# Row attention on one core: maxima rows ahead in the transfer queue, loads in two halves, and TensorE's shifted products ahead of its scores

## The reference

```python
def _L0_xattn_ref(q, k, v):
    b, d, m = q.shape            # 64, 64, 256
    h = N_HEAD                   # 8 heads of 8 rows
    qh = q.reshape(b * h, d // h, m)
    kh = k.reshape(b * h, d // h, -1)
    vh = v.reshape(b * h, c // h, -1)
    qk = jnp.einsum('bdm,bdn->bmn', qh, kh) * scale
    sm = jax.nn.softmax(qk, axis=-1)
    ret = jnp.einsum('bmn,bcn->bcm', sm, vh)
    return ret.reshape(b, c, m)

x = x + _L0_xattn_ref(_layernorm(x, axis=-1), ctx_2048, ctx_2048)
```

## Time and profile before

| what | value |
|---|---|
| median of 3 runs | 2517.65 us (2515.28 to 2520.46) |
| profiled execution | 2522.49 us, span of its trace 2520.6 us |
| mean granted TensorE clock | 0.792 of full |
| busy over the span | PE 60%, DVE 64%, ACT 42%, POOL 24% |
| row attention, first score to last result added | 146.6 us to 608.4 us |

### The profile page before, as it was taken

The page is one execution under the profiler, slowest core; times in us unless marked ns, Lnnn a source line. Parts: engine busy times, 40 slices in busy tenths (PEclk is TensorE's granted clock), DMA queues, the critical chain, the costliest instruction groups (busy, mean ns, idle before and its releaser), DMA issues. The chain is left out here.

```text
span 2520.6 us, 34997 instructions
## 1 busy us (share of the span) xinstructions
PE 1518.6 (60%) x11260; PEld 924.7 (37%) x11260; DVE 1622.3 (64%) x3141; ACT 1062.1 (42%) x1453; POOL 613.7 (24%) x862
## 2 busy tenths in 40 slices
PE   1069999994995787874334343279999367620022
PEld 1035555552774544542112112135555233310011
DVE  6457777773453477675777887445555487856787
ACT  4427667673221334344355455323333377710022
POOL 4312233332002223223333433201010011105500
PEclk9999999996998788897555556689999688855555
DMA  6635555542001221211000000001100100003001
GB/s 179 173 77 117 119 120 119 119 114 76 1 0 30 51 60 40 47 43 56 10 1 1 0 0 0 21 29 31 29 25 23 51 1 0 1 21 61 6 26 41
DMA packets 94652, 120.97 MB, mean 48 GB/s; under 512 B 25868, under 2 KB 78284, under 8 KB 89932
## 3 DMA queue, kind: packets, MB, share of 16 engines
q1 hardware_dynamic: 94540, 119.56, 19.0%
HBM read 79.75 MB, written 22.09 MB: 40 GB/s over the span
## 5 line engine op out<-in xcount | busy, mean ns | idle before, releaser
L571 DVE TENSOR_REDUCE ratt_nmax<-ratt_psS 128x2 f32<-128x512 f32 x512 | 319.9, 684 | 112.6 <-PE ratt_psS L463 112.0
L537 ACT ACTIVATE ratt_E<-ratt_psT 128x1024 f32<-128x1024 f32 x256 | 255.6, 1022 | 123.9 <-PE ratt_psT L485 123.8
L463 PE MATMUL ratt_psS<-ratt_K,ratt_Q 72*128 72x256 bf16 x1024 | 210.7, 291 | 54.4 <-DMA ratt_K<-ratt_ones 48.5
L485 PE MATMUL ratt_psT<-ratt_Q,ratt_K 75*128 75x256 bf16 x1024 | 202.6, 283 | 15.2 <-DMA ratt_Q<-ratt_rows 14.8
L498 PE MATMUL ratt_psO<-ratt_E,ratt_V 128*32 128x256 f32 x2048 | 144.8, 403 | 0.7 <-ACT ratt_E L537 0.7
L463 PEld LDWEIGHTS ratt_psS<-ratt_K,ratt_Q 72*128 72x128 bf16 x1024 | 82.3, 101 | 154.2 <-issue 94.0
L1833 PE MATMUL nffn_psH<-nffn_W,nffn_QT 128*128 128x512 bf16 x128 | 57.7, 601 | 114.6 <-DVE nffn_H L1797 95.8
L485 PEld LDWEIGHTS ratt_psT<-ratt_Q,ratt_K 75*128 75x128 bf16 x1024 | 102.4, 101 | 36.2 <-issue 16.8
L1316 PE MATMUL gatt_psA<-gatt_DA,gatt_same 128*128 128x512 f32 x128 | 89.1, 786 | 25.3 <-DVE gatt_DB L1201 25.3
L1135 POOL TENSOR_TENSOR gatt_DA<-gatt_own,gatt_a 128x1024 f32<-128x1024 f32 x32 | 61.5, 1935 | 143.4 <-PE gatt_psA L1319 90.4
L1756 POOL TENSOR_TENSOR nffn_H<-nffn_H,nffn_gam 128x1024 f32<-128x1024 f32 x32 | 93.1, 2937 | 7.4 <-DVE nffn_H L1788 7.4
(11 more groups left out here) (451 smaller groups left out, 4124.3 us busy)
## 6 DMA issues: line engine op xcount, KB each, us to landing
ratt_Q<-z_parts SPq DMA_DIRECT2D x32, 576.0 KB
ratt_K<-context_parts SPq DMA_DIRECT2D x96, 192.0 KB
gatt_V<-in_ctx_dram SPq DMA_DIRECT2D x16, 512.0 KB, 6.9
z_parts<-prep_ZS SPq DMA_DIRECT2D x48, 128.0 KB, 2.7
context_parts<-prep_CS SPq DMA_DIRECT2D x48, 128.0 KB
head_sums<-ratt_O SPq DMA_DIRECT2D x64, 72.0 KB
all_X<-in_x_dram SPq DMA_DIRECT2D x8, 512.0 KB, 4.8
prep_C<-in_ctx_dram SPq DMA_DIRECT2D x8, 512.0 KB, 5.6
```

Source lines behind the costliest of these rows:

```text
L463: mm = nc.tensor.matmul(psS[:, RING[h], c * D:(c + 1) * D], Q9[0:R, buf, h, k % 2, c * P:(c + 1) * P], K9[0:R, buf, h, k % 2, :], start=Tr ...
L485: mm = nc.tensor.matmul(psT[:, p % 2, e, c, :], K9[0:RM, buf, h, u, c * P:(c + 1) * P], Q9[0:RM, buf, h, u, :], start=True, stop=True)
L537: nc.scalar.activation(E[:, 2 * b + p // 2, 2 * (p % 2):2 * (p % 2) + 2], psT[:, p % 2], ACT.Exp, scale=SCALE).then_inc(exped, 1)
L571: nc.vector.tensor_reduce(nmax[:, k % 2, h, :], psS[:, RING[h]].rearrange("p (c t) -> p c t", c=2), AX.X, ALU.max, negate=True).then_inc(m ...
```

## The change

On SP the row comes first in each slot; the load is halved, with Q in the odd slot n and K in the even slot n+1 (group of units n+3 and n+4 as before, so K is issued one slot later than before); `inverses_out` moves from the pair's fourth slot to its next one (slot 4a+12), `back` from slot 4a+12 to 4a+14, behind that slot's K load. DVE's reciprocal goes from slot 4a+10 to 4a+11, POOL's `scale_and_add` from 4a+13 to 4a+15. The ones are all issued before the first load. On PE, each head's shifted product stands ahead of the score of the other unit's head.

```diff
                 def slot(i, k):
                     n = i * 8 + k
-                    row_there = held(sp, n) if is_unit(n - 1) else None
-                    if k % 2 == 1 and past(n, 5) and is_unit(n + 3):
-                        free = held(sp, n * 4 - 4 * LAG)
-                        pair = held(sp, i * 2 + (k + 3) // 4)
-                        sp.wait_ge(shifted, free)
-                        load(pair, (k + 3) // 2 % 2, (k + 3) // 2 % BUFS)
...
+                    if is_unit(n - 1):
+                        bring_row(held(sp, n), (k - 1) // 2 % BUFS, (k - 1) % 2)
+                    if past(n, 5):
+                        g = (k + 3) // 2 if k % 2 else (k + 2) // 2
+                        if is_pair(i * 2 + g // 2):
+                            if k % 2:
+                                free, pair = held(sp, n * 4 - 4 * LAG), held(sp, i * 2 + g // 2)
+                                sp.wait_ge(shifted, free)
+                                load_q(pair, g % 2, g % BUFS)
+                            else:
+                                load_k(held(sp, i * 2 + g // 2), g % 2, g % BUFS)
                     c = (k - 8) // 4
...
+                    if k % 4 == 0 and is_pair(i * 2 + c - 1):
+                        inverses_out(held(sp, (i * 2 + c - 1) * P), held(sp, i * 2 + c), (c - 1) % 2)
+                    if k % 4 == 0 and is_pair(i * 2 + c):
+                        out(held(sp, i * 2 + c), held(sp, (i * 2 + c) * 4 + 4), c % 2)
+                    if k % 4 == 1 and is_pair(i * 2 + c):
+                        sums_back(held(sp, (i * 2 + c) * 16), c % 2, held(sp, (i + c // 2) * 64 + 64))
+                    if k % 4 == 2 and is_pair(i * 2 + c - 1):
+                        back(held(sp, (i * 2 + c - 1) * 16), (c - 1) % 2, held(sp, (i + (c - 1) // 2) * 16 + 16))
...
                 for buf in range(BUFS):
                     sp.dma_start(K9[R:RM, buf].rearrange("p h u m -> p (h u) m"), spread(ones[:], 1, 2 * NH0)).then_inc(
                         ones_in, 16)
-                    load(buf // 2, buf % 2, buf)
-                slots(sp, slot, UNITS + 9)
+                for g in range(BUFS):
+                    load_q(g // 2, g % 2, g)
+                    load_k(g // 2, g % 2, g)
+                slots(sp, slot, UNITS + 11)
...
-                    c = (k - 13) // 4
-                    if k % 4 == 1 and is_pair(i * 2 + c):
+                    c = (k - 15) // 4
+                    if k % 4 == 3 and is_pair(i * 2 + c):
                         scale_and_add(i * 2 + c, c % 2, i + c // 2)
...
                         for e in range(2):
+                            if is_unit(m):
+                                shift(i, k, p, e)
                             if is_unit(n):
                                 score(i, k, 2 * p + e)
-                            if is_unit(m):
-                                shift(i, k, p, e)
...
-                    c = (k - 10) // 4
-                    if k % 4 == 2 and is_pair(i * 2 + c):
+                    c = (k - 11) // 4
+                    if k % 4 == 3 and is_pair(i * 2 + c):
                         dve.wait_ge(d_in[c % 2], (i + c // 2) * 16 + 16)
```

More of the change, by code:

```diff
@@ L319, in _, with load_q, load_k @@
             def _(sp):
-                def load(pair, b, buf):
+                def load_q(pair, b, buf):
                     q = zq.rearrange("s r a (b h) u m -> (s r) a b (h u m)", b=2)[:, bass.ds(pair, 1), b, :]
-                    k = ck.rearrange("r s a (b h) u m -> (r s) a b (h u m)", b=2)[:, bass.ds(pair, 1), b, :]
                     sp.dma_start(Q9[0:R, buf].rearrange("p h u m -> p (h u m)"), spread(
                         q.rearrange("p a m -> p (a m)"), 1, 3)).then_inc(group_in[buf], 16)
+                def load_k(pair, b, buf):
+                    k = ck.rearrange("r s a (b h) u m -> (r s) a b (h u m)", b=2)[:, bass.ds(pair, 1), b, :]
                     for part in range(3):
@@ L361, in slot @@
                     n = i * 8 + k
-                    row_there = held(sp, n) if is_unit(n - 1) else None
-                    if k % 2 == 1 and past(n, 5) and is_unit(n + 3):
-                        free = held(sp, n * 4 - 4 * LAG)
-                        pair = held(sp, i * 2 + (k + 3) // 4)
-                        sp.wait_ge(shifted, free)
-                        load(pair, (k + 3) // 2 % 2, (k + 3) // 2 % BUFS)
-                    ago = k % 4
-                    c = (k - 8) // 4
[L370 to L386, removed]
@@ L387, in slot @@
-                    if row_there is not None:
-                        bring_row(row_there, (k - 1) // 2 % BUFS, (k - 1) % 2)
+                    if is_unit(n - 1):
[9 more added lines that the diff above has]
+                                load_k(held(sp, i * 2 + g // 2), g % 2, g % BUFS)
@@ L441, in slot @@
                         split_max(n - 1, (k - 1) % 2)
-                    c = (k - 13) // 4
-                    if k % 4 == 1 and is_pair(i * 2 + c):
+                    c = (k - 15) // 4
+                    if k % 4 == 3 and is_pair(i * 2 + c):
                         scale_and_add(i * 2 + c, c % 2, i + c // 2)
-                slots(pool, slot, UNITS + 10)
+                slots(pool, slot, UNITS + 12)
             @block.tensor
@@ L582, in _ @@
                 nc.vector.tensor_copy(identb[:], ident[:]).then_inc(ident_set, 1)
-                slots(dve, slot, UNITS + 7)
+                slots(dve, slot, UNITS + 8)
 def pipeline(engine, front, back):
```

## The result

The changed kernel takes 2526.67 us (median of 7 runs, 2522.97 to 2537.0), the kernel before 2517.65 us beside it; the ratio is 1.0048 with a 95% interval of 1.0029 to 1.0067. So it is slower, as forecast and within the range of 2512 to 2600, but by 7 to 17 us (the medians lie 9 us apart, the ratio says 12) and not by 41. The wait that was forecast is there, twelve times and at the slots named. With what surrounds it, it cost 46.1 us, six tenths of the 75.6 in the sum.

The account below looks back on a forecast made before the run. PE's own stream was taken as the limit, with 31.7 us lost around late rows. The terms -31.7 + 75.6 + 4 - 7.3 + 1 = +41.6 us gave 2559 us from 2517.65, with 8 in 10 between 2512 and 2600.

Parts of the forecast that it names:

- Rows first, loads halved: On SP: rows no longer stand behind `back`'s wait or whole loads; PE's six waits and their clock go, -31.7 us.
- `back` behind K: POOL gets `num` late, so PE waits 3.5 us in twelve turns, with 2.8 us of lower clock each: +75.6 us.
- K one slot later: In even slots K's data end close to the first score's due time: 0.3 us in 12 slots, +4 us.
- Shifted product first: On PE: the new order moves everything by 0.22 us once and the slot stays 6.19 us: 0.
- Ones first: At the start PE begins at about 130 and slot 3 at 154 instead of 161.3: -7.3 us, -1 to -12.
- Tail: At the block's end the next to last pair's `back` stands between the last pair's `sums_back` and `inverses_out`: +1 us.
- Rival A: At POOL's wait: `num` is in time and no turn is late; -38 us, 2480 us, chance 0.12.
- Rival B: On the queue: `den` and `num` don't wait behind K; 1.8 us wait, 1.7 clock, +4, 2522 us, chance 0.12.
- Rival C: On PE: frequent waits leave the clock at 1.2 GHz for most of two slots; +74, 2592 us, chance 0.18.

Follow-up runs that it names:

- e1: The changed kernel with POOL's `scale_and_add` one POOL slot later, behind the split that a turn of PE waits for: 2481.11 us, ratio 0.9872.
- e8: The changed kernel with only the sum into X moved behind the next split, the product left in its POOL slot: 2491.34 us, ratio 0.9901.
- e9: The changed kernel with one more product of the same size, unused, on POOL ahead of the split: 2554.61 us, ratio 1.0162.
- e5: The kernel of e1 with PE's order of before, scores ahead of shifted products: 2481.56 us, ratio 0.9856.
- e2: The changed kernel with PE's order of before, scores ahead of shifted products: 2525.81 us, ratio 1.0048.
- e3: The kernel before with only PE's order changed, shifted products ahead of scores: 2517.04 us, ratio 1.0012.
- e4: The changed kernel with the ones issued in turn with the four first loads, as before: 2535.07 us, ratio 1.0081.
- e7: The kernel before with only the ones issued ahead of the four first loads: 2505.69 us, ratio 0.9948.
- r1: The changed kernel as it is, timed and profiled once more: 2527.41 us, ratio 1.0054.
- e6: The changed kernel with `back` (`den` and `num`) issued ahead of its slot's K load instead of behind it: 2551.14 us, ratio 1.0143.

## Why the prediction was wrong

By its own steps:

- *Rows first, loads halved, -31.7.* Right. In e1, where nothing else disturbs, all 31.7 us are back. Rows first and the halved loads were never run apart, so which of the two did it is open.
- *`back` behind K, 12 waits, +75.6.* The mechanism, the slots and the count were right; **this term was mis-sized**, at 46.1 us. Of the 29.5 us between, the wait itself is 42.0 - 27.5 = 14.5: `num` came at t = 10.55 instead of 11.3, mostly because `den` was issued at t = 4.34 and not at 4.9, while the distance from there to POOL's start was 6.21 us where 6.4 was taken (on the mean of the twelve `num` came at 10.3, 6.0 us behind `den`); and the 3.5 us ran from the due time of the turn, whereas PE waits less than it is late (2.63 us of 2.80 at slot 24) and makes up 0.34 us in the next slot. The other 15.0 us are the clock: 2.8 us were put behind each wait, 33.6 in all, and 18.6 were found. This is the step that failed: 12 x (3.5 + 2.8) took a wait of 3.5 us where 2.3 came, and a fall of the clock behind every one where only five had one. The six waits that this came from were 1.5 to 3.1 us long and all had a fall behind them. At the new place the clock fell behind 5 of 12 waits of 2.3 us, behind none of 0.9 (e8), and behind all twelve of 3.6 (e9). The length alone doesn't explain it, as the last section shows: waits for rows of the same 2.3 us always had a fall.
- With waits as long as forecast the loss is about as forecast: e9 has 3.6 us, twelve falls and 70.4 us.
- *K one slot later, +4.* Next to 0 in this kernel: between slots 10 and 62 one wait of 0.3 us for K. It comes in time for a score that is due at 8.8, and e5 shows that 0.22 us less would be too little.
- *Shifted product first, 0.* Right (e2, e3, e5).
- *Ones first, -7.3.* The right sign and place, -8.8 at the first turn with shifted products (157.61 against 166.43) and -11.1 at slot 10, the rest because PE's products reach their full rate sooner: a pair of them takes 0.63 us until 161.6 in the changed kernel and until 175.6 before, 0.38 after that. The profile gives the granted clock as 1.00 on both sides of these times, so that the slow stretch is the clock isn't shown. e4 and e7 give the same 11 us. It was within the stated -1 to -12.
- *Tail, +1.* From slot 62 to the next stage it is 42.57 us against 41.75: +0.8.

The sum by measured terms is -31.7 + 46.1 - 11.1 + 0.8 = +4.1 us at the block's end, where the two profiled executions have +4.2 (609.33 to 613.49). Against the +41.6 of the forecast, 29.5 us are missing by the mis-sized term, 4 by K and 3.8 by the start. The medians have 9 us. The profiled executions of the changed kernel are the fastest of their runs (2522.97 of 2522.97 to 2537.0; 2520.84 of 2520.84 to 2532.14), so more falls of the clock in the other runs could explain the difference, and the kernel without waits spreads over 4 us where the changed one spreads over 14. But the mean granted clock of each run doesn't bear it out: it follows the time in e2's runs (0.802 at 2515.38 us, 0.794 at 2534.92) and not in the changed kernel's (0.793 at 2522.97 us and at 2532.7). What fills the other 5 us is open.

Rival A, in which `num` is in time, is e1 by another road: -38 us was forecast for it and -33 measured against the kernel before timed beside it. Rival B's sum, +4 us, is what the block shows, but by luck: its wait of 1.8 us was too short (2.3 measured) and its `num` at 9.6 too early (10.3 measured on the mean), while its 1.7 us of clock behind each wait is near the 1.6 measured on the mean, which are five falls of 3.6 us and seven waits without one. Rival C, a clock that stays low behind every wait, did not come.

## What to carry to other kernels

When a stage of a chain is moved later on one queue, follow its data to the engine that waits for them in order, and ask what stands behind that wait: here a sum into X with slots to spare held back a split that every fourth turn of PE needed, and one slot more for it is the whole difference between 0.5% slower and 1.3% faster. A wait's cost isn't its length times its count: here the lower clock behind it came not at all, sometimes or always, by the wait's length and by its place in the program. A mean of six waits at one place was a poor price for twelve at another, even at the same length; give such a term a range from no fall to a fall behind each. Look at the start of a stage for small transfers queued behind large ones; four transfers of 24 KB held PE for 16 us here.

## What the runs showed of the hardware that I had not expected

The granted clock, read from the traces in stretches of 1 us behind each wait of PE in the otherwise dense stream, answered like this:

| the wait, and the kernels | length, us | clock fell to 0.50 |
|---|---|---|
| turn, for POOL's split (e8) | 0.8 to 1.0 | 0 of 12 |
| the same (changed, r1, e2, e4) | 1.8 to 2.6 | 5, 5, 3 and 5 of 12 each |
| the same (e9) | 3.3 to 3.9 | 12 of 12 |
| shifted product, for a row (before, e3, e7) | 0.4 to 1.2 | 0 of 4 |
| the same | 1.4 to 3.1 | 16 of 16 |
| score, for K (e6) | 1.5 and 2.3 | 0 of 2 |
| the same | 1.9 to 3.7 | 10 of 10 |

At one place the share of falls grows with the length, but a wait for a row of 1.43 us had a fall where turn waits of 2.6 had none, and the places of the falls differ between two executions of one kernel. So the length doesn't decide alone; what else does, no run here isolates. Two of the cases, each the wait and then a window behind it (e7 in slot 22, clock 0.50; e6 in slot 19, clock 1.00):

```profile
283.13 0.39 PE L486 MATMUL ratt_psT<-ratt_Q,ratt_K 75*128 75x256 bf16 x2 [1.43 <-DMA ratt_Q<-ratt_rows]
```

```profile
286.00:292.00 6.00, 6.00 (x38) 3.08 (x35) 2.77 (x4) 2.78 (x4) 1.54 (x6) 0.50 0.62 130
```

```profile
264.43 0.39 PE L460 MATMUL ratt_psS<-ratt_K,ratt_Q 72*128 72x256 bf16 x2 [2.25 <-DMA ratt_K<-context_parts]
```

```profile
265.00:275.00 10.00, 9.86 (x106) 6.12 (x104) 8.40 (x14) 8.11 (x10) 2.93 (x12) 1.00 0.42 113
```

A fall behind the turn waits of 1.8 to 2.6 us cost 1.2 to 4.3 us in the slot behind it. Behind the 3.6 us waits it was mostly 1.8 to 2.1 us, so each cost less, but there were more of them; why it is shorter there, no run here shows.
